# Expert slots of a mixture-of-experts layer: the gathered x moved through a stage buffer, and an expert's weights in one 2 MB transfer

## The reference

```
x = x + attention(layernorm(x), ctx)                 # 8 x 256 tokens of 512 elements
h = layernorm(x)                                     # 2048 tokens
w, sel = top 4 of 32 experts for each token          # softmax weights, made to sum to 1
large: for token t and expert e: (silu(h Wg[e]) * (h Wu[e]) * w[t,e]) Wd[e]        # inner width 192
small: the same with cWg, cWu, cWd of expert e // 2                                # inner width 128
x = x + large + 0.05 * small
```

## Time and profile before

| | |
|---|---|
| median of 3 runs | 1057.66 us (1057.39 to 1059.92) |
| the profiled execution | 1061.51 us, of which 1059.8 us is the span from first to last instruction |
| the part `experts` begins, first instruction of POOL | 455.47 us into the span |
| PE busy over the span | 986.3 us (93%) |
| mean granted TensorE clock | 0.965 of full speed |

### The profile page before, as it was taken

One profiled execution on the slowest core, in us unless ns is written; L12 is line 12 of the kernel. 1 busy time (PEld: TensorE's weight loads), 2 busy tenths in 40 slices (PEclk: granted clock), 3 DMA queues, 4 the chain that ended last, 5 costly groups with the idle time before them and its releaser, 6 DMA issues.

```text
span 1059.8 us, 18705 instructions
## 1 busy us (share of the span) xinstructions
PE 986.3 (93%) x5163; PEld 726.0 (69%) x5164; DVE 524.5 (49%) x1233; ACT 314.0 (30%) x631; POOL 300.3 (28%) x399
## 2 busy tenths in 40 slices
PE   7789999999999988449999999999999999999994
PEld 6557666676665535337878778777787777877872
DVE  4677677777677726933333333333333333333331
ACT  2245465555555535901111111111111111111110
POOL 3011101011120001223434344343443434434432
PEclk9999999999999989669999999999999999999997
DMA  6163234231431008227897998989888899889563
GB/s 208 45 166 77 66 91 102 86 86 56 121 80 51 32 31 304 105 72 174 219 244 181 249 253 219 243 218 254 199 221 215 211 259 249 213 208 251 111 114 68
DMA packets 102603, 168.23 MB, mean 159 GB/s; under 512 B 15520, under 2 KB 65824, under 8 KB 98208
## 3 DMA queue, kind: packets, MB, share of 16 engines
q1 hardware_dynamic: 36624, 103.11, 31.0%
q0 software_dynamic: 17792, 43.30, 21.6%
q10 hardware_dynamic: 48144, 21.25, 7.4%
HBM read 101.29 MB, written 29.36 MB: 123 GB/s over the span
## 4 chain that ended last, share of the span: by engine, by line
PE 54%; DMA 1%; issue 1%; DVEq 0%; DVE 0%; ACTq 0%; POOL 0%; ACT 0%; SPq 0%; POOLq 0%
PE y_ps L1650 19%; PE g_ps L1633 17%; PE u_ps L1633 16%; PE at_ps L1642 2%; DMA xg<-xd,gidx 0%; DMA xT<-xb 0%; ACTq L1542 0%; POOL out_x L1515 0%; DVEq L1618 0%; DVE xb L1596 0%; ACT sg L1547 0%; DVEq L1583 0%; ACT yb L1553 0%; DVE aT L1579 0%; DVEq L1619 0%
## 5 line engine op out<-in xcount | busy, mean ns | idle before, releaser
L1650 PE MATMUL y_ps<-W,aT 128*128 x468 | 216.3, 598 | 3.6 <-DVE aT L1579 3.6
L1633 PE MATMUL g_ps<-W,xT 128*128 x624 | 192.2, 451 | 13.3 <-DMA xT<-xb 13.0
L1515 POOL DMA_INDIRECT out_x<-yb,yidx x78 | 125.3, 1606 | 278.1 <-ACT yb L1553 194.4
L518 DVE TENSOR_REDUCE mx<-s 128x2 f32<-128x512 f32 x256 | 163.4, 682 | 59.3 <-PE s L709 58.6
L397 ACT ACTIVATE pt<-stp 128x512 f32<-128x512 f32 x256 | 139.1, 596 | 148.1 <-PE stp L723 147.4
L1633 PE MATMUL u_ps<-W,xT 128*128 x624 | 180.7, 432 | 0.0
L1633 PEld LDWEIGHTS g_ps<-W,xT 128*128 128x128 f32 x624 | 168.3, 311 | 15.2 <-issue 15.1
L1633 PEld LDWEIGHTS u_ps<-W,xT 128*128 128x128 f32 x624 | 171.0, 308 | 0.0
L1650 PEld LDWEIGHTS y_ps<-W,aT 128*128 128x128 f32 x468 | 89.6, 192 | 85.7 <-issue 79.6
L1596 DVE STREAM_TRANSPOSE xb<-xg 128x512 f32<-128x512 f32 x80 | 89.1, 1114 | 79.5 <-DMA xg<-xd,gidx 76.2
L1547 ACT ACTIVATE sg<-g_ps 128x320 f32<-128x320 f32 x78 | 34.2, 438 | 305.8 <-PE u_ps L1633 305.8
(11 more groups left out here) (197 smaller groups left out, 842.9 us busy)
## 6 DMA issues: line engine op xcount, KB each, us to landing
W<-in_wts SPq DMA_DIRECT2D x32, 1280.0 KB
W<-in_wts SPq DMA_DIRECT2D x32, 768.0 KB
xT<-xb ACTq DMA_DIRECT2D x320, 64.0 KB
qst<-q SPq DMA_DIRECT2D x42, 256.0 KB, 5.0
xs<-in_x SPq DMA_DIRECT2D x8, 512.0 KB, 3.6
ctxT<-in_ctx SPq DMA_DIRECT2D x8, 512.0 KB, 4.0
out_x<-xs SPq DMA_DIRECT2D x16, 256.0 KB, 2.3
kst<-k SPq DMA_DIRECT2D x48, 64.0 KB, 2.1
```

The costliest lines, as they stand in the source:

```text
L518: dve.tensor_reduce(mx[j // CH % 2][:, h:2 * G:G], s1[r][:, :, :], AX.X, ALU.max)\
L1515: pool.indirect_dma_start(out[:, :], bass.IndirectOffsetOnAxis(yidx[p][:, :], 0), yb[p][:, :], None, compute_op=ALU.add).then_inc(y_added, ...
L1633: m = pe.matmul(ps_[p][:, 0:IW], xT[p][:, :, c], W[:, bass.ds(buf, 1), (2 * c + g) * IW:(2 * c + g + 1) * IW] .rearrange("p a f -> p (a f) ...
L1650: m = pe.matmul(y_ps[:, :], aT[p][:, c, :], W[:, bass.ds(buf, 1), GW + c * D:GW + (c + 1) * D].rearrange("p a d -> p (a d)"), start=(c == ...
```

## The change

Weights: `PIECES` has one piece, so an expert is one DMA of 2 MB, issued when the last slot of the expert that held the buffer has gone through down.

Moving x: the gathered rows of slot s are transposed by `turn` in another order (read with a stride of four floats, written contiguously), moved by the same four DMAs into `stage[p]`, and then copied by DVE (`place`) into `xT[p]`, whose layout is now chunk by chunk, so that PE reads its weights contiguously. The arrays of Wg and Wu in DRAM are laid out to match. `x_move`, `turn` and `gather` run one slot further ahead. The x of slot 0 doesn't go this way: PE transposes it, and ACT copies it to `xT[0]`. The weight of the expert is picked in two steps, `weight_next` (with `turn`) and `weight_now`. PE gets 16 transposes without use (`keep_clock`) at the start of `experts` and again in front of the last down. One explicit load of an activation table in `route` goes, and the first four gathers take their indices straight from the table.

```
-PIECES = ((0, GW), (GW, WW))
+PIECES = ((0, WW),)
...
                     last = sp.value_load(cum_i[0:1, bass.ds(i * NW + p - NW, 1)], min_val=1, max_val=NS)
                     sp.wait_ge(slots_done, last)
                     load_piece(sp, wts, W, w_loaded, i, p, 0)
-                    sp.wait_ge(slots_done, last + 1)
-                    load_piece(sp, wts, W, w_loaded, i, p, 1)
                     arrived(i if p else i - 1, (p - 1) % NW)
...
-            act.preload_act_table_set("natural_log_exp_and_others")
...
             def x_move(s, p):

-                act.wait_ge(turned, s + 1)
-                if not (isinstance(s, int) and s < 2):
-                    act.wait_ge(gu_full, s - 1)
+                act.wait_ge(turned, s)
+                if not (isinstance(s, int) and s < 3):
+                    act.wait_ge(copied, s - 2)
                 for i in range(QB):
-                    act.dma_start(xT[p][:, i * Q:(i + 1) * Q, :].rearrange("m r c -> m (r c)"),
+                    act.dma_start(stage[p][:, i, :, :].rearrange("m c r -> m (c r)"),
                                   xb[p][i * Q:(i + 1) * Q, :]).then_inc(x_ready[p], DMA)
...
             def slot(s, p, first=False):
+                x_move(s + 3, 1 - p)
                 silu(s, p)
-                x_move(s + 2, p)
                 if not first:
                     y_evac(s - 1, 1 - p)
...
-            def weights_of(s, p):
+            def weight_next(s, p):

                 e = dve.value_load(slot_e[0:1, bass.ds(s, 1)], min_val=0, max_val=E_ - 1)
                 dve.wait_ge(x_loaded[p], (s - p) * (DMA // 2) + DMA)
+                dve.tensor_copy(wn[p][:, :], xg[p][:, bass.ds(e + D, 1)]).then_inc(wn_ready, 1)
+
+            def weight_now(s, p):
+
+                dve.wait_ge(wn_ready, s + 1)
                 if not (isinstance(s, int) and s < 2):
                     dve.wait_ge(a_ready, s - 1)
-                dve.tensor_copy(wt[p][:, 0:1], xg[p][:, bass.ds(e + D, 1)]).then_inc(wt_ready, 1)
+                dve.tensor_copy(wt[p][:, 0:1], wn[p][:, :])
+                dve.tensor_scalar(wt[p][:, 1:2], wn[p][:, :], SMALL, None, ALU.mult).then_inc(wt_ready, 1)
...
             def turn(s, p):

-                dve.wait_ge(x_loaded[p], (s - p) * (DMA // 2) + DMA)
+                weight_next(s, p)
+                if not (isinstance(s, int) and s < 3):
+                    dve.wait_ge(x_ready[p], moved(s - 2, p))
+                dve.transpose(xb[p][:, :], xg[p][:, 0:D].rearrange("t (c q j) -> t j c q", c=C, j=QB)).then_inc(turned, 1)
+
+            def place(s, p):
+
+                dve.wait_ge(x_ready[p], moved(s, p))
                 if not (isinstance(s, int) and s < 2):
-                    dve.wait_ge(x_ready[p], moved(s - 2, p))
-                dve.transpose(xb[p][:, :].rearrange("p (j r c) -> p j c r", r=Q, c=C), xg[p][:, 0:D]).then_inc(turned, 1)
+                    dve.wait_ge(gu_full, s - 1)
+                dve.tensor_copy(xT[p][:, :, :].rearrange("m c (i r) -> m c i r", i=QB),
+                                stage[p][:, :, :, :].rearrange("m i c r -> m c i r")).then_inc(copied, 1)
...
+            def slot(s, p, first=False):
+                if not first:
+                    at_evac(s - 1, 1 - p)
+                weight_now(s + 1, 1 - p)
+                place(s + 1, 1 - p)
+                turn(s + 3, 1 - p)
+                gated(s, p)
...
                         add(i * 2 + p - 1, 1 - p)
-                        gather(i * 2 + p + 4, p)
+                        gather(i * 2 + p + 5, 1 - p)
...
+            keep_clock(16)
+            transpose_x0()
             slot(0, 0, first=True)
...
             transpose_a(last + 1, 1)
+            keep_clock(16)
             down(last + 1, 1, pe.value_load(slot_buf[0:1, bass.ds(last + 1, 1)], min_val=0, max_val=NW - 1))
```

More of the change, by code:

```diff
@@ L1078, in _ @@
         def _(sp):
-            for n in range(2):
-                load_piece(sp, wts, W, w_loaded, 0, 0, n)
+            load_piece(sp, wts, W, w_loaded, 0, 0, 0)
             for t in range(LATE, NT):
@@ L1086, in _ @@
             for p in range(1, NW):
-                for n in range(2):
-                    load_piece(sp, wts, W, w_loaded, 0, p, n)
+                load_piece(sp, wts, W, w_loaded, 0, p, 0)
             for p in range(2):
@@ L1439, in experts @@
         xg = [sb(f"xg{i}", [P, XW], F32) for i in range(2)]
+        wn = [sb(f"wn{i}", [P, 1], F32) for i in range(2)]
         wt = [sb(f"wt{i}", [P, 2], F32) for i in range(2)]
         xb = [sb(f"xb{i}", [P, D], F32) for i in range(2)]
-        xT = [sb(f"xT{i}", [P, P, C], F32) for i in range(2)]
+        stage = [sb(f"stage{i}", [P, QB, C, Q], F32) for i in range(2)]
+        xT = [sb(f"xT{i}", [P, C, P], F32) for i in range(2)]
         sg = [sb(f"sg{i}", [P, IW], F32) for i in range(2)]
@@ L1516, in add @@
                                         compute_op=ALU.add).then_inc(y_added, DMA)
-            for s in range(4):
+            for s in range(6):
                 gather(s, s % 2)
-            gather(4, 0)
             add(0, 0)
-            gather(5, 1)
+            gather(6, 0)
             n, last = count(pool)
@@ L1606, in _ @@
                 dve.memset(a[p][:, IW:IP], 0.0)
-            for p in range(2):
-                turn(p, p)
-                weights_of(p, p)
+            weight_next(0, 0)
+            weight_now(0, 0)
+            turn(1, 1)
             turn(2, 0)
[L1611 to L1616, removed]
+            def slot(s, p, first=False):
[5 more added lines that the diff above has]
+                gated(s, p)
+            slot(0, 0, first=True)
+            slot(1, 1)
             n, last = count(dve)
@@ L1620, in _ @@
                     for p in range(2):
[L1621 to L1624, removed]
+                        slot(i * 2 + p, p)
             at_evac(last + 1, 1)
@@ L1628, in _, with transpose_x0, keep_clock @@
         def _(pe):
+            def transpose_x0():
+                pe.wait_ge(x_loaded[0], DMA)
+                for c in range(C):
+                    m = pe.transpose(xt_ps[:, c * P:(c + 1) * P], xg[0][:, c * P:(c + 1) * P], ident[:, :])
+                m.then_inc(xt_full, 1)
+            def keep_clock(n):
+                for _ in range(n):
+                    pe.transpose(xt_ps[:, 0:P], ident[:, :], ident[:, :])
             def gate_up(s, p, buf):
-                pe.wait_ge(x_ready[p], moved(s, p))
+                if isinstance(s, int) and s == 0:
+                    pe.wait_ge(x0_ready, 1)
+                else:
+                    pe.wait_ge(copied, s)
                 for ps_, g in ((g_ps, 0), (u_ps, 1)):
                     for c in range(C):
-                        m = pe.matmul(ps_[p][:, 0:IW], xT[p][:, :, c],
+                        m = pe.matmul(ps_[p][:, 0:IW], xT[p][:, c, :],
                                       W[:, bass.ds(buf, 1), (2 * c + g) * IW:(2 * c + g + 1) * IW]
```

49 lines of the change are left out of this document (29 added, 20 removed).

## The result

| | before | after |
|---|---|---|
| median | 1057.53 us (4 runs) | 1120.47 us (4 runs, 1109.77 to 1127.49) |
| ratio | | 1.0558, 95% interval 1.0518 to 1.0598 |
| profiled execution; its span | 1061.51; 1059.8 | 1119.29; 1117.5 |
| start of slot 0 (first `at_ps` row) | 474.21 | 473.44 |
| start of slot 77, the last | 1040.87 | 1101.64 |

The ratios here leave out runs that lie more than 1.5% above the fastest of their kernel, 1127.49 here and 1109.69 in experiment 6.

The account below looks back on a forecast made before the run. PE was taken to bound the slots before. Of 77 periods, 28 behind a load (37.8) and 49 not (7.4), with start +0.3, end -2.5 and route -0.5, gave +42.5 on 1057.7: 1100 us, range 1062 to 1130.

Parts of the forecast that it names:

- The order on ACT and DVE: Slot loop through at_evac, turn, four DMA issues, silu and gated: period 7.48 us, 0.15 more than now.
- the second rival: Queues share the DMA engines and the longer load delays nothing further: 1067 us (1060 to 1080), chance 0.20.
- PE's own work of 7.22: PE's slot time if nothing waits: g loses 0.11 us through contiguous x weights.
- The faster rival: The loop over ACT is shorter than PE's work, slots without a load bound by PE at 7.22: 1046 us, chance 0.13.
- One transfer of 2 MB: The load makes the next slot's gather land late: period 8.68 us, 1.35 more than now, in 28 slots.
- w = 3.55: Time from slot start to the start of `wn`, set behind a load by the gather's landing; 2.35 otherwise.
- Sharing or passing ahead: Whether the extra load bytes share the engines with the gather or pass ahead of it; landing taken as 3.7 us.
- the third rival: The load passes ahead of everything: w = 4.85, period 9.98 behind a load, 1137 us, chance 0.14.
- The start: Slot 0: gather 0 is issued earlier, but silu(0) stands behind x_move(3): +0.3 us.
- the route: In `route` one activation table load of 1.28 us goes: -0.5 us taken, between 0 and 1.28 on the path.
- The end: Last y: the 16 transposes fill part of the gap ahead, y 2.74 instead of 5.48 us: -2.5, bounds 0 and -2.7.
- The clock: PE's clock over the slots: no fall expected through gaps of 0.3 to 1.5 us in each slot.

Follow-up runs that it names:

- experiment 6: Kernel after with weights in two transfers (1280 and 768 KB) issued together, and x_move behind silu on ACT: 1098.07 us, ratio 1.0363.
- experiment 7: Kernel after without any weight load in the loop, all slots computing with the weights of the first four experts: 1066.11 us, ratio 1.0089.
- experiment 3: Kernel after with x_move behind silu on ACT and weights in two pieces a slot apart: 1044.28 us, ratio 0.9877.
- experiment 5: Kernel after with weights in two transfers (1280 and 768 KB), both issued where the one is: 1107.33 us, ratio 1.0481.
- experiment 2: Kernel after with x_move behind silu on ACT, load still one transfer of 2 MB: 1120.9 us, ratio 1.0611.
- 8: Kernel with x_move behind silu and two pieces a slot apart, without the idle transposes (`keep_clock`) at both places: 1044.5 us, ratio 0.988.
- experiment 4: Kernel before with the weights in one transfer of 2 MB, nothing else changed: 1109.08 us, ratio 1.0502.
- experiment 1: Kernel after with weights in two pieces a slot apart (1280 KB, then 768 KB), as before: 1085.7 us, ratio 1.0266.
- experiment 9: Kernel after with each expert in two transfers issued together, cut by partitions (64 rows of 16 KB each): 1260.75 us, ratio 1.1912.

## Why the prediction came out as it did

The time of 1120 was inside the range, 20 us above the 1100; the loads cost 20.8 more than forecast (54.4 against 33.6), which makes up the difference; smaller misses cancel. The mechanism was right in one half. In the other, late gathers were foreseen, but over half of what the trace shows (29.6 of 51.6 us) is a held issue that the prediction didn't have, and its own term measured 15.7. That the time came so near is in part luck.

- **The order on ACT and DVE: right.** Forecast 7.48, measured 7.46. Copies and waits came within 0.06 us: `xT<-stage` started at 1.46 (forecast 1.44) and took 0.43, less even than the lower bound; `wn` started at 2.41 (2.35). Silu starts 0.04 behind the fourth issue. By itself, with no load in the way, this leaves 1066 (experiment 7), the 1067 of the second rival, but that rival's premise on the loads was wrong, and experiment 7 meets its time only because it has no loads.
- **PE's own work of 7.22: right.** It is 7.21 as soon as nothing waits (experiment 3). The faster rival asked for a loop below 7.22; x_move behind silu cuts the loop, and with the old pieces the time is its 1046 less 2.
- **One transfer of 2 MB: the step that failed.** It said that the load makes the gather of the slot behind late, w = 3.55, and that slots behind a load take 8.68: 28 x 1.20 = 33.6 us over the loop. The runs show 54.4 (after against experiment 7; 51.6 by the trace). In the slot itself, where the prediction put no cost, ACT's fourth issue is held: 29.6 us. Late turns are only 15.7; a slot that is stretched to 8.7 gives the gather that much more time. Where the issue isn't held (experiment 5) the late turns are 31.0, near the 33.6. So the term was that of a kernel without held issues. The hold was no visible cost before: there the moves stood behind silu, and a late issue was hidden beside y. I had summed four issues of 2.54 from a slot without a load, and never asked whether an engine's DMA issue can itself wait for another queue's transfer. A hint stood in the trace of before: 8 of its issues on ACT are over 1 us, 1.29 at most, all 5.3 to 6.6 us behind a load's issue. A slip in the sum beside this: 768 KB at 304 GB/s are 2.6 us and not 2.5, which moves the upper bound alone.
- **Sharing or passing ahead.** The page "DMA: Bandwidth & Descriptors" of the Trainium skill (Queues, rings and completion order) says that each DMA engine takes turns between its queues packet by packet. No run here tests the rule itself, but what the prediction drew from it, that a longer load holds up the gather no further, is not what the traces show: a gather issued 0.38 us behind the load landed after 10.1 us (experiment 2), 0.9 us before that load did. What the third rival describes is therefore seen where gather and load are issued together; in the kernel after the gather's issue lies 4 us behind the load's, and the slot behind a load was 8.0 and not 9.98.
- **The start**: forecast +0.3 and, with the route, -0.2; measured -0.8. The twelve issues in front of the table load ended at 470.91 (forecast 472.0) and silu and `a` followed as counted.
- **The end**: forecast -2.5, measured -3.0. The forecast was that y runs at the full clock, 2.74. In the kernel after it took 3.64 in place of 5.48, which is 1.8 us, and it began 1.1 earlier in its slot (3.07 us after the start, 4.15 before), a term that the forecast didn't have. The last add still follows `yb` there. In the kernels of experiments 3 and 8 it makes no difference how fast y is (2.84 or 4.53): PE's gap ahead of y is under 2 us, and POOL's index copy for the last add comes no earlier than 7.3 us after the start.
- **The clock**: it stayed at 0.99 over the slots, as expected. Two slots have a slow g, 4.03 and 3.67 us in place of 2.34, behind waits of PE of 2.25 and 1.93 us, at a granted clock of 0.66 and 0.64 (645.03 to 650.00 and 934.46 to 939.00); the second took 8.98 us with no late turn and no held issue. Behind the other gaps, of 2.58 at most, g kept its 2.34.

The costs don't add: the transfer costs 51 us in the kernel before (experiment 4), 77 with the moves behind silu (2 against 3), and 35 with the moves in front (after against 1). A reading that fits, and that no run tests alone: with the moves in front every slot is longer and has slack for the gather, and with PE as the bound a late gather is paid in full, and the slow clock behind a long wait comes on top (24 of the 77 in experiment 2). The order costs 41 us with small pieces (1 against 3) and nothing with the large one (after against 2).

What stays open: why one transfer of 2 MB, and to a lesser degree one of 1280 KB, holds an issue on another engine's queue, while two transfers with the same bytes at the same moment don't. The place of the held issue is not fixed. With 2 MB it begins 5.2 to 7 us behind the load's issue in nearly every case and ends 7 to 8 us behind it, and it is the fourth of four in the kernel after but the second or third in experiments 2 and 4; in no run was the first held. The length of a row does not decide it (experiment 9). The bytes of a single transfer alone don't either: 1280 KB by themselves hold issues up to 1.34 (experiment 1), and the same 1280 KB with 768 KB right behind them none above 0.87 (experiment 5). What resource it is wasn't measured. In experiment 2 the chain over add and gather was read from one trace and not tried by itself.

## What to carry to other kernels

When a step is moved in front of another on an engine that issues DMAs, sum its issues at their longest in the profile, beside a transfer in flight, and not at their mean: what was hidden behind the last use is now on the path. Before pieces of a transfer are joined, ask who issues and who lands within its 9 us; here 2 MB in one slot cost 35 to 77 us, and the same bytes a slot apart were free once ACT's list put silu first. A good edit can be hidden by its companions: undo them one at a time, and in pairs. Where PE comes to wait for several microseconds, count the slow clock behind the wait as well: 24 us in experiment 2.

## What the runs showed of the hardware that I had not expected

- A DMA issue on ACT takes up to 2.27 us in place of 0.64, mostly about 5.4 us behind the issue of a 2 MB transfer on SP's queue (4.1 or 5.2 us behind one of 1280 KB in experiment 1, up to 1.34). With two transfers together (1280 and 768 KB) none is above 0.87.
- Two transfers of 64 partitions x 16 KB, issued together, are complete some 12.4 us after the first issue, where one of 128 partitions with all the bytes takes 8.8 in the loop (experiment 9). The kernel became 140 us slower.
- An indirect gather of 128 rows, issued 0.38 us behind a 2 MB load, lands after 10.1 us; without a load it is 3.75.
- With `xT` contiguous, the weight load of a g pass takes 195 ns, and 191 for u, on the page of the kernel after:

```profile
L1669 PEld LDWEIGHTS u_ps<-W,xT 128*128 128x128 f32 x624 | 119.4, 191 | 50.4 <-issue 1.7
...
L1669 PEld LDWEIGHTS g_ps<-W,xT 128*128 128x128 f32 x624 | 115.3, 195 | 40.9 <-issue 5.1
```

  Before they are 311 and 308 ns. What came of it in a slot is 0.12 us of its 7.33.
